# Moving the gram products, the gathers' waits and the layers of an embedding-interaction kernel, and adding idle products

## What is computed

```python
e = jnp.stack([tbl_0[ids[:, 0]], tbl_1[ids[:, 1]], ..., tbl_26[ids[:, 26]]], axis=1)   # 512 x 27 x 128
dot_products = jnp.einsum('bnd,bmd->bnm', e, e)
z = dot_products[:, c, r]                       # c, r = the 351 places below the diagonal
h = jnp.concatenate([z.reshape(512, -1), dense_ctx], axis=1)   # 512 x 367
h = jnp.maximum(h @ W_top1 + b_top1, 0.0)       # 512 wide
h = jnp.maximum(h @ W_top2 + b_top2, 0.0)       # 256 wide
y = h @ W_top3                                  # 512 x 1
```

## Time and profile before

| | us |
|---|---|
| timed, median of 3 runs | 109.17 |
| timed, lowest and highest | 109.1 and 109.28 |
| profiled execution, first to last instruction (span) | 123.6 |

### The profile page before, as it was taken

One profiled execution on the slowest core, in us unless ns is written; L12 is line 12 of the kernel. 1 busy time (PEld: TensorE's weight loads), 2 busy tenths in 40 slices (PEclk: granted clock), 3 DMA queues, 4 the chain that ended last, 5 costly groups with the idle time before them and its releaser, 6 DMA issues.

```text
span 123.6 us, 3473 instructions
## 1 busy us (share of the span) xinstructions
PE 106.3 (86%) x1496; PEld 86.1 (70%) x1496; DVE 70.0 (57%) x98; ACT 67.2 (54%) x112; POOL 68.1 (55%) x71
## 2 busy tenths in 40 slices
PE   6998799899999899999329993789458999997992
PEld 6534487687887687788219883669448999797891
DVE  6799999999999999999900050015001060103401
ACT  4596929899999999995200052025301144531442
POOL 3777888888888888887744166416560665000000
PEclk9999999999999999999985599558975699999999
DMA  3896366966984574711210101110200011000000
GB/s 79 262 237 190 101 204 146 293 198 155 302 235 111 172 229 108 205 48 42 54 52 17 31 29 42 27 48 21 66 24 27 21 48 41 23 5 5 5 0 1
DMA packets 5305, 12.06 MB, mean 98 GB/s; under 512 B 1765, under 2 KB 2277, under 8 KB 5290
## 3 DMA queue, kind: packets, MB, share of 16 engines
q1 hardware_dynamic: 3282, 7.75, 22.0%
q0 software_dynamic: 1984, 4.07, 12.8%
q10 hardware_dynamic: 24, 0.02, 0.1%
HBM read 11.83 MB, written 0.00 MB: 96 GB/s over the span
## 4 chain that ended last, share of the span: by engine, by line
PE 68%; DVE 16%; issue 13%; ACT 1%; DVEq 0%
PE ring L512 21%; PE gram_ps L539 12%; DVE marks L651 10%; PE gram_ps L512 8%; PE ring L592 5%; PE ids_ps L574 4%; PE ring L523 4%; DVE low L628 3%; PE ids_ps L567 2%; PE ids_ps L523 2%; PE ring L574 2%; PE ring L602 2%; PE ids_ps L592 1%; DVE pick L610 1%; PE ids_ps L553 1%
## 5 line engine op out<-in xcount | busy, mean ns | idle before, releaser
L422 POOL DMA_INDIRECT rows<-tbl,ids_sb x62 | 67.1, 1082 | 36.3 <-issue 15.9
L651 DVE TENSOR_TENSOR marks<-ids_ps,row_no 125x1024 fp32r<-125x1024 f32 (+2 forms) x39 | 43.5, 1148 | 0.0
L512 PE MATMUL ring<-marks,high 125*128 125x512 f32 (+1 forms) x64 | 26.6, 416 | 1.7 <-issue 1.6
L539 PE MATMUL gram_ps<-rowsT 128*27 128x27 f32 x1024 | 15.8, 206 | 11.4 <-issue 11.2
L512 PE MATMUL ring<-marks,low 125*128 125x512 f32 (+1 forms) x64 | 25.2, 394 | 0.0
L539 PEld LDWEIGHTS gram_ps<-rowsT 128*27 128x27 f32 x1024 | 13.3, 118 | 14.7 <-issue 14.0
L512 PEld LDWEIGHTS ring<-marks,high 125*128 125x128 f32 x64 | 12.8, 200 | 7.1 <-issue 4.6
L724 ACT ACTIVATE away<-ids_ps,row_no 125x512 f32<-125x512 f32 (+1 forms) x22 | 14.0, 715 | 4.7 <-PE ids_ps L466 4.1
L628 DVE TENSOR_TENSOR low<-raw,high 125x512 fp32r<-125x512 f32 (+1 forms) x23 | 16.2, 705 | 0.0
L672 DVE STREAM_TRANSPOSE gram<-gram_ps 128x416 f32<-128x416 f32 (+1 forms) x8 | 4.6, 612 | 18.1 <-PE gram_ps L539 18.1
L512 PEld LDWEIGHTS ring<-marks,low 125*128 125x128 f32 x64 | 12.9, 202 | 1.6
(11 more groups left out here) (61 smaller groups left out, 116.5 us busy)
## 6 DMA issues: line engine op xcount, KB each, us to landing
raw<-tbl SPq DMA_DIRECT2D x9, 448.0 KB
raw<-tbl SPq DMA_DIRECT2D x2, 560.0 KB
rows<-tbl,ids_sb POOLq DMA_INDIRECT x62
w_sb<-w SPq DMA_DIRECT2D x2, 256.0 KB
w_sb<-w SPq DMA_DIRECT2D x1, 512.0 KB
raw<-tbl SPq DMA_DIRECT2D x9, 52.0 KB
raw<-tbl SPq DMA_DIRECT2D x2, 224.0 KB
w_sb<-w SPq DMA_DIRECT2D x1, 192.0 KB
```

What stands on the lines that cost most here:

```text
L422: nc.gpsimd.indirect_dma_start(out=rows[0:n, i % ROW_BUFS, s, :], out_offset=None, in_=tables[PLACES[s]], in_offset=bass.IndirectOffsetOnA ...
L512: last = nc.tensor.matmul(bank[:, 0:n], part[:, i % SPLIT_BUFS, c * D:(c + 1) * D], mark_of(unit, c), start=c == 0 and part is high, stop= ...
L539: last = nc.tensor.matmul(gram_ps[s * STRIP:s * STRIP + F, g, 0:F], places, places, start=True, stop=True)
L651: nc.vector.tensor_tensor(marks_of(unit)[:, c0 - c1:, :], index.to_broadcast([TP, c1 - c0, n]), which.to_broadcast([TP, c1 - c0, n]), ALU. ...
```

## The change

The table of the order is another one after the first 31 steps: all four quarters of a gram stand in a row in all four tiles, and layers stand between the grams. The table of the gathers' waits ends otherwise: gather 38 waits for `products 1` (gram 0 done), gather 42 for `products 2`, gather 50 for `products 3`, and there are no other entries from 38 on; the waits for the `rows` buffers stay. There is a new kind of step, `idle i`, which takes a ring bank and issues 8 or 16 products of `still`. Everything else is as it was; the ring's places follow from the table.

```diff
+IDLE = (8, 16)
...
-find 10 1, gram 0 0, gram 0 1, find 11 0, gram 0 2, gram 0 3, find 11 1, turn 2 0, turn 2 1, gram 1 0
...
-l2 1 1, pairs 2 1, pairs 2 2, turn 3 2, l3 1, l1 2 0, turn 3 3, l1 2 1, gram 3 0, gram 3 1, l1 2 2
...
+find 10 1, gram 0 0, gram 0 1, gram 0 2, gram 0 3, find 11 0, find 11 1, turn 2 0, pairs 0 0
...
+l3 1, pairs 2 0, pairs 2 1, pairs 2 2, l1 2 0, l1 2 1, l1 2 2, turn 3 1, l1 2 3, l1 2 4, idle 0
+turn 3 2, idle 1, turn 3 3, gram 3 0, gram 3 1, gram 3 2, gram 3 3, l2 2 0, l2 2 1, pairs 3 0
...
-32 marks_used 30, 34 turned 6, 36 marks_used 35, 38 marks_used 38, 40 turned 9, 42 gram_part 2
-44 gram_part 3, 46 marks_used 50, 48 gram_part 5, 50 products 2, 52 l1_done 1, 54 gram_part 7, 56 paired 6
-58 products 3, 60 l1_done 7
+32 marks_used 30, 34 turned 6, 36 marks_used 35, 38 products 1, 42 products 2, 50 products 3
...
-                    else:
+                    elif kind != "idle":
                         pe.wait_ge(taken, MOVED.index(("find", i, 1) if kind == "find" else held[-1]) + 1)
...
+                elif kind == "idle":
+
+                    warm(IDLE[i], use_ring(step))
```

More of the change, by code:

```diff
@@ L143 @@
 find 7 1, turn 1 0, find 8 0, find 8 1, find 9 0, turn 1 1, find 9 1, find 10 0, turn 1 2, turn 1 3
-find 10 1, gram 0 0, gram 0 1, find 11 0, gram 0 2, gram 0 3, find 11 1, turn 2 0, turn 2 1, gram 1 0
-gram 1 1, gram 1 2, pairs 0 0, pairs 0 1, turn 2 2, pairs 0 2, gram 1 3, turn 2 3, l1 0 0, l1 0 1
-l1 0 2, l1 0 3, l1 0 4, gram 2 0, gram 2 1, gram 2 2, pairs 1 0, turn 3 0, pairs 1 1, pairs 1 2
-l2 0 0, l2 0 1, gram 2 3, l3 0, l1 1 0, turn 3 1, l1 1 1, l1 1 2, l1 1 3, l1 1 4, l2 1 0, pairs 2 0
-l2 1 1, pairs 2 1, pairs 2 2, turn 3 2, l3 1, l1 2 0, turn 3 3, l1 2 1, gram 3 0, gram 3 1, l1 2 2
-l1 2 3, l1 2 4, gram 3 2, gram 3 3, l2 2 0, l2 2 1, pairs 3 0, pairs 3 1, l3 2, pairs 3 2, l1 3 0
-l1 3 1, l1 3 2, l1 3 3, l1 3 4, l2 3 0, l2 3 1, l3 3
+find 10 1, gram 0 0, gram 0 1, gram 0 2, gram 0 3, find 11 0, find 11 1, turn 2 0, pairs 0 0
+pairs 0 1, pairs 0 2, turn 2 1, gram 1 0, gram 1 1, gram 1 2, gram 1 3, l1 0 0, l1 0 1, l1 0 2
+l1 0 3, l1 0 4, pairs 1 0, pairs 1 1, pairs 1 2, turn 2 2, l2 0 0, l2 0 1, l1 1 0, l1 1 1, l1 1 2
+turn 2 3, l1 1 3, l1 1 4, l3 0, gram 2 0, gram 2 1, gram 2 2, gram 2 3, l2 1 0, l2 1 1, turn 3 0
+l3 1, pairs 2 0, pairs 2 1, pairs 2 2, l1 2 0, l1 2 1, l1 2 2, turn 3 1, l1 2 3, l1 2 4, idle 0
+turn 3 2, idle 1, turn 3 3, gram 3 0, gram 3 1, gram 3 2, gram 3 3, l2 2 0, l2 2 1, pairs 3 0
+pairs 3 1, pairs 3 2, l3 2, l1 3 0, l1 3 1, l1 3 2, l1 3 3, l1 3 4, l2 3 0, l2 3 1, l3 3
 """
```

## The result

| | us |
|---|---|
| before, median of 4 runs | 109.19 (109.1 to 109.28) |
| after, median of 4 runs | 124.14 (122.77 to 126.16) |
| ratio after / before | 1.132, 95% interval 1.126 to 1.1385 |
| profiled execution of after | 124.24, span 122.4, mean granted clock 0.972 |

The change makes the kernel 15 us slower. The ratio is one of fast runs alone, without the run of 126.16 us, whose granted clock was the lowest. The forecast was 5.3 us slower, with a range to 118.5: right in its sign, and far too small. An execution of after takes 1.84 us more than its span (124.24 against 122.4).

A forecast was written before the change was run, and what follows sets the result against it. The profile was taken as bound by TensorE's grams stalling beside gathers, stalls assumed absent from timed runs. +6.7 for gather 61, -1.35 for the moved layer, 0 for idle products: +5.3, 114.5 us; range 109.2 to 118.5.

The forecast's parts named there:

- I take the stalls as the profile's own.: Gaps of 11.2 us in TensorE's grams beside gathers were taken as absent from timed runs; both kernels laid out without them.
- A gram takes 2.5 us where nothing disturbs it.: Unit price on TensorE at full clock: 2.5 us for each whole gram.
- The rest of the sum: Gather 61 starts at 94.2 instead of 87.5, +6.7 us; -1.35 for the layer moved, 0 for idle products: +5.3 us.
- the 1.35 us gained by the layer ahead: Layer 1 of tile 2 stands wholly ahead of gram 3, taking 1.35 us out of the tail.
- The waits as a chain: Gathers 38, 42, 50 wait for whole grams; gathers queued behind follow at 1.25 us, delaying gather 61 and gram 3 by 6.7 us.
- The new wait before `turn 2 2`: TensorE reaches this turn at 71.3 and waits for gather 43's rows until 72.2, put at 0.6 us.
- The idle products at no cost: The 24 idle products, 5.4 us, lie in TensorE's waits between gram 2 and gram 3 and cost 0.
- Rival (3): The clock falls between gram 2 and the end, costing 3.4 or 4.3 us: 118 to 118.8 us; chance 0.15.
- Rival (1): The stalls beside gathers are real and the change removes them: 10.6 us less, 98.6 us; chance 0.14.
- Rival (4): Gathers come every 0.95 us without the profiler: +8.0, 117.2 us; upper end of the forecast, inside its chance of 0.54.
- Rival (2): Part of the stalls, 4.4 us, is in timed runs and the change saves it: 110.1 us; chance 0.15.
- The mark of the theory: The span of after is shorter than before's (110 to 115 against 123.6) while the timed runs are slower.

The follow-up runs named there:

- b1: The kernel before, unchanged, run again for a second profile: 109.44 us, span 107.6.
- c2: The changed kernel with no waits of gathers from 38 on except for buffers, and no idle products: 112.96 us, ratio 1.0345 to before.
- d1: The changed kernel without idle products and with only the third wait for grams (gather 50 for gram 2): 125.34 us, ratio 1.1402 to before.
- b4: The changed kernel without its 24 idle products, all three waits kept: 124.89 us, ratio 1.1403 to before.
- c4: The kernel before with 512 more of the gram's small products at its very end, where no gather runs: 137.26 us.
- d4: The kernel before with 512 small products at its end and one 128-wide product of the cleared tile after every eighth: 151.6 us.
- b2: The changed kernel with the table of gathers' waits of before, idle products kept: 120.33 us.

## Why the prediction was wrong

- **"I take the stalls as the profile's own."** This step failed. Two kinds of gap stood in one trace. Those beside the gathers in the earlier trace rows do not come again in b1. But the reasoning went from "they are not in a timed run" to "a timed run has no gaps", and the second is false: b1 has 2.6 us of them and after 8.4. The 14.4 us between span and time were a sign that the one recorded execution was untypical, not that the profiler stretches each of them: b1's span is 1.84 us below its time.
- **"A gram takes 2.5 us where nothing disturbs it."** This is the term of the sum that was mis-sized: three grams stand between gather 38 and gather 50, and one behind gather 61. The row behind it is 128 records in 1.23 us, half a gram. It held for half a gram and was doubled. A gram in one piece is 512 instructions, and measured 4.8 us for gram 0 in after. Nothing in the rows read covered more than 128 records without a pause, so the bound from above should have been open there. A gap of 0.66 us in the last gram of the recorded profile, with no gather near, pointed to it, and I left it out of the sum. These are the rows:

```profile
111.00 0.52 PE L539 MATMUL gram_ps<-rowsT 128*27 128x27 f32 x38
112.18 0.97 PE L539 MATMUL gram_ps<-rowsT 128*27 128x27 f32 x90 [0.66 <-issue]
```

  With the first half's 128 the stop is behind record 166, as in c2, where the same instructions stand before it.
- **The rest of the sum was right in kind.** Gather 61 started 13.6 us later than in b1 (102.21 against 88.65), where 6.7 was laid out. Three gaps of 2.30, 2.12 and 1.86 us before gather 50 and 1.65 us of layer 1 at the half clock make 7.9 us, about what separates 88.44 from the 80.5 laid out. (By its own terms the layout has a slip: from 72.2 the steps up to the end of gram 2 add up to 8.2 us, so gather 50 belongs at 80.7.) b1's own gather 61 was 1.15 us later than laid out. From gather 61 to the end it is 20.2 us in after and 19.0 in b1; the 1.35 us gained by the layer ahead are eaten by gram 3's gap (2.11) and the half clock after it (1.65). These three would make 2.4 us and not 1.2: b1 has a gap of 0.34 us in its own gram 3, and its last turn starts 2.9 us after gather 61, in after 2.5; the last 0.4 us are not accounted for. 13.6 + 1.2 is the 14.8 us between the spans.
- **The waits as a chain** held: only the third one decides (d1), 1.25 us a gather, and the turns of tile 3 wait for gathered rows. The new wait before `turn 2 2` did not come: gather 43 starts at 74.58, and TensorE, late by its grams, gets to that turn at 77.81 without waiting. **The idle products at no cost** held within the spread (b4).
- **Rival (3), the clock,** happened, 1.65 us twice, but together with the main case, and behind gaps in grams, not in waits for gathers. Rival (1) is out: the stalls of the earlier trace rows are not in b1, and the gaps that are there are not removed by the waits. Rival (4) is out: gathers keep 1.25 us. Rival (2) has the right point (some gaps lie in a timed run) and the wrong sign for after.
- **The mark of the theory**, a span shorter than before's with slower runs, was seen (122.4 against 123.6), and shows nothing, since the 123.6 was untypical. I should have named the span that the laid-out before implies, 104.8, as the thing to test; it was 107.6.

A page of the Trainium skill bears on the mechanism: "Runtime: NRT & Kernel Launch", section "Instruction fetch mechanics", says that instructions are fetched in blocks of 16 KiB, 256 of them, while the current block runs, and that the cost is mostly hidden. The block size agrees with c4. That it is hidden does not: in c4 TensorE stood still 1.7 to 2.5 us for each block. It was hidden in d4, where a block lasts an estimated 4.7 us (36 instructions in 0.66 us).

## What to carry to other kernels

Count instructions, not only work: where many small products follow one another, TensorE is bound by the delivery of its instructions. Here it got 256 in 3.6 us, after a first stretch of 330 to 490 (166 to 246 records with their loads), whose length went by where the page boundary fell. The same products spread among wide ones left no gap (d4), though each wide one then cost 0.2 us more. A price read from a short burst must not be multiplied up to a long one. And before a profile is taken as the kernel's, its span has to fit the timed runs; a span longer than the time says that this execution is not the one that was timed.

## What the runs showed of the hardware

- TensorE's instructions came as 16 KB pages; in a dense run of float32 products (two loads and two matmuls each) one page lasted 1.25 us at 2.4 GHz (1.7 at 1.2 GHz) and the next came 3.64 us after the one before, going on about 1.2 to 1.4 us after the page's transfer had ended (c4, and the four gaps of after).
- The stops stood at the same records whatever the gathers did, and 96 more instructions ahead of them moved a stop from record 166 to 246 (c2, b4, after, b2).
- A gather beside small products stretched 225 records from 2.14 to 3.52 us (after, c2), while sixteen records of layer 2 took 1.95 us both beside gathers (b1, at 80.70) and without them (b1, at 102.93).
- A 128-wide float32 product between small ones took 0.42 us, against 0.224 in a row of its kind (d4).
- The granted clock fell to 0.50 for 3.4 us behind two of after's four gaps (2.12 and 2.11 us) and not behind the other two (2.30 and 1.86), in c2 behind one of 1.42 us and not behind one of 2.04, and not once in b1, whose gaps are 1.1 us at most. So the length of a gap does not decide it by itself.
- One execution of before, the one recorded first, has a span 16 us longer than b1's, with products issued three or four at a time beside gathers. What it was stays open.
